# A two-hop graph product with layer norm: the products of steps 1 to 5 are issued one step earlier in TensorE's order

## The reference, cut to what matters

```python
adj = adjacent_mat((A + A.T) * 0.5)      # add the identity, scale rows and columns by deg ** -0.5
y = Coefficient2 @ adj                   # Coefficient2 is A, that is the raw input adj
y = y @ x
out = layernorm(x + y)
```

## Time and profile before

| | |
|---|---|
| median of three runs | 429.55 us |
| the profiled execution's own time | 428.08 us |
| its span | 426.3 us |
| PE busy | 393.6 us (92%) |
| DVE busy | 241.3 us (57%) |
| ACT busy | 111.6 us (26%) |
| POOL busy | 74.0 us (17%) |
| mean granted clock of PE | 0.974 of full speed |

### The profile page before, as it was taken

The page is one execution under the profiler, slowest core; times in us unless marked ns, Lnnn a source line. Parts: engine busy times, 40 slices in busy tenths (PEclk is TensorE's granted clock), DMA queues, the critical chain, the costliest instruction groups (busy, mean ns, idle before and its releaser), DMA issues.

```text
span 426.3 us, 5406 instructions
## 1 busy us (share of the span) xinstructions
PE 393.6 (92%) x1822; PEld 325.6 (76%) x1822; DVE 241.3 (57%) x463; ACT 111.6 (26%) x195; POOL 74.0 (17%) x109
## 2 busy tenths in 40 slices
PE   3479999997799699999999999999999999999994
PEld 3467788885588488888888888888888888888883
DVE  0656777773704402222266227777777777777752
ACT  1124444432603402222222222222222222222210
POOL 3466878752000000000000000000000000000000
PEclk9659999999999999999999999999999999999999
DMA  8999855430004736226232256565555555655500
GB/s 241 303 315 288 243 165 185 136 100 2 0 2 98 174 74 148 49 51 147 50 100 50 49 127 152 137 151 138 146 137 149 139 146 137 150 138 151 122 25 25
DMA packets 73969, 54.76 MB, mean 128 GB/s; under 512 B 3552, under 2 KB 62048, under 8 KB 73952
## 3 DMA queue, kind: packets, MB, share of 16 engines
q1 hardware_dynamic: 73952, 54.54, 49.8%
HBM read 41.94 MB, written 4.19 MB: 108 GB/s over the span
## 4 chain that ended last, share of the span: by engine, by line
issue 73%; PE 14%; DVE 7%; DMA 2%; SPq 2%; POOL 1%; ACT 0%; POOLq 0%; DVEq 0%
PE ps L412 3%; PE ps L391 3%; PE ps L393 3%; PE ps L392 3%; DVE lots_r L674 2%; DMA lots_s<-adj 2%; PE ps L420 1%; DVE u_lo L686 1%; POOL rstd L382 1%; DVE lots_s L633 1%; DVE store L633 1%; DVE deg L648 0%; SPq L284 0%; PE ps L435 0%; SPq L274 0%
## 5 line engine op out<-in xcount | busy, mean ns | idle before, releaser
L393 PE MATMUL ps<-z,w_lo 128*128 128x512 f32 x256 | 99.7, 389 | 0.0
L391 PE MATMUL ps<-z,w_hi 128*128 128x512 f32 x256 | 99.7, 389 | 0.0
L392 PE MATMUL ps<-z,w_hi 128*128 128x512 f32 x256 | 99.7, 389 | 0.0
L391 PE MATMUL ps<-u_hi,w_hi 128*128 128x512 f32 x176 | 69.4, 394 | 4.1 <-DVE z_raw L700 4.1
L616 ACT ACTIVATE w_hi<-turned 128x512 fp32r<-128x512 f32 x64 | 39.8, 632 | 122.9 <-DVE turned L741 122.9
L393 PE MATMUL ps<-u_hi,store_lo 128*128 128x512 f32 x176 | 69.3, 394 | 0.0
L392 PE MATMUL ps<-u_lo,w_hi 128*128 128x512 f32 x176 | 69.1, 392 | 0.0
L741 DVE STREAM_TRANSPOSE turned<-strips 128x512 f32<-128x512 f32 x64 | 65.5, 1069 | 0.0
L382 POOL TENSOR_TENSOR rstd<-var_eps,mhalf 128x1 f32<-128x1 f32 x16 | 8.8, 548 | 303.6 <-DVE var_eps L791 303.6
L700 DVE SCALAR_TENSOR_TENSOR z_raw<-ps,dinv_half,z_raw 128x512 fp32r<-128x512 f32 x16 | 11.9, 750 | 86.4 <-ACT z_raw L572 86.4
L391 PEld LDWEIGHTS ps<-z,w_hi 128*128 128x128 f32 x256 | 48.1, 188 | 10.0
(11 more groups left out here) (78 smaller groups left out, 432.7 us busy)
## 6 DMA issues: line engine op xcount, KB each, us to landing
strips<-adj SPq DMA_DIRECT2D x64, 256.0 KB, 4.5
z<-z_raw SPq DMA_DIRECT2D x64, 128.0 KB, 2.4
u_x<-x SPq DMA_DIRECT2D x16, 256.0 KB, 4.7
x_res<-x SPq DMA_DIRECT2D x16, 256.0 KB, 2.6
out<-y_out SPq DMA_DIRECT2D x16, 256.0 KB, 2.1
lots_s<-adj SPq DMA_DIRECT2D x13, 256.0 KB, 4.6
store<-adj SPq DMA_DIRECT2D x2, 512.0 KB, 5.7
col_slot<-adj SPq DMA_DIRECT2D x1, 896.0 KB, 9.8
```

What stands on the lines that cost most here:

```text
L391: nc.tensor.matmul(out_, hi, mov_hi, start=first, stop=False)
L392: nc.tensor.matmul(out_, hi, mov_lo, start=False, stop=False)
L393: return nc.tensor.matmul(out_, lo, mov_hi, start=False, stop=last)
```

## The change

A table `DONE_BY` says how many units PE has issued by the end of each step. Before, it was none by the end of step 1, then 5, 10, 15 and 20 by the ends of steps 2 to 5. Now it is 5, 10, 13, 17 and 21, and 25 by the end of step 6, as before; from there on the orders are alike. In step k the units of blocks up to k-2 still go between the chunks (`units_left`); those of block k-1 go behind the last chunk and mirror of the step (`late`). That makes 5 late units in step 1, 5 in step 2, 3 in step 3, 2 in step 4 and 1 in step 5.

On DVE, `lot_low` and `u_low` of block 0 (and the first `first_low`) stand behind the second add of step 1 and no longer behind its degrees; in steps 2 to 5 `lot_low` and `u_low` of block k-1 stand ahead of the degrees. The columns of step 1 take turns in both transposing banks, so that a chunk waits for the add of the chunk before the last.

```diff
@@ -250,6 +250,15 @@
         def main_parts(k):
             return sum(main_part(j) is not None for j in range(k))
 
+
+        DONE_BY = {1: 5, 2: 10, 3: 13, 4: 17, 5: 21}
+
+        def done_by(k):
+            return DONE_BY.get(k, max(0, (G + 1) * (k - 1)))
+
+        def bank_of(k, i):
+            return i % 2 if k < 2 else 0
+
         def hi_of(n):
             return w_next if n == 1 else w_hi[:, (n + 1) % 2 if n == 0 else n % 2]
 
@@ -406,10 +415,10 @@
                     last.then_inc(s_tc, 1)
 
             def transpose_cols(k, i, b0, b1):
-                pe.wait_ge(s_add, chunk_at(k) + i)
+                pe.wait_ge(s_add, chunk_at(k) + i - (k == 1 and i > 0))
                 for b in range(b0, b1):
                     src = row(k, b, b + 1) if b == k else col(k, b, b + 1)
-                    last = nc.tensor.transpose(tp[0][:, b - b0], src[:, 0], ident[:])
+                    last = nc.tensor.transpose(tp[bank_of(k, i)][:, b - b0], src[:, 0], ident[:])
                 last.then_inc(s_tc, 1)
 
             def mirror(k, n, i, b0, b1):
@@ -463,10 +472,14 @@
 
             pe.wait_ge(s_ident, 2)
             first_step()
+            units = [(j, m) for j in range(NB) for m in range(G + 1)]
             for k in range(1, NB):
                 cols_left = list(enumerate(chunks_of(k)))
                 mirrors_left = [(mirror_at(k - 1) + n, m) for n, m in enumerate(mirrors_of(k - 1))] if 2 <= k <= NR else []
-                units_left = list(range(G + 1)) if k >= 2 else []
+                quota = DONE_BY.get(k, (G + 1) * (k - 1)) - done_by(k - 1)
+                ripe = max(0, (G + 1) * (k - 1) - done_by(k - 1))
+                units_left, late = units[:min(quota, ripe)], units[min(quota, ripe):quota]
+                del units[:quota]
                 pe.wait_ge(s_in[k], 16 * ((k < NR) + (k < NB - 1) + 1))
                 summed = False
                 while cols_left or mirrors_left or units_left:
@@ -477,10 +490,12 @@
                         n, (i, b0, b1) = mirrors_left.pop(0)
                         mirror(k - 1, n, i, b0, b1)
                     if units_left:
-                        multiply_unit(k - 2, units_left.pop(0))
+                        multiply_unit(*units_left.pop(0))
                     if not summed:
                         col_sums(k)
                         summed = True
+                for unit in late:
+                    multiply_unit(*unit)
                 if k > NR:
                     mirror_corner(k - 1)
             for m in range(G + 1):
@@ -629,7 +644,7 @@
             def add_chunk(k, i, b0, b1):
                 dve.wait_ge(s_tc, chunk_at(k) + i + 1)
                 w = row(k, b0, b1)
-                bank = tp[i % 2 if k == 0 else 0]
+                bank = tp[bank_of(k, i)]
                 nc.vector.scalar_tensor_tensor(w, bank[:, 0:b1 - b0], 1.0, w, ALU.mult, ALU.add,
                                                accum_out=part_sum[:, k, i:i + 1]).then_inc(s_add, 1)
 
@@ -704,6 +719,13 @@
             for k in range(NB):
                 for i, (b0, b1) in enumerate(chunks_of(k)):
                     add_chunk(k, i, b0, b1)
+                    if k == 1 and i == 1:
+                        lot_low(0)
+                        u_low(0)
+                        first_low(0)
+                if 2 <= k < 6:
+                    lot_low(k - 1)
+                    u_low(k - 1)
                 degrees(k)
                 if k == 0:
                     nc.vector.tensor_tensor(c0[:, 0], c0[:, 0], ident2[:], ALU.add).then_inc(s_d0, 1)
@@ -714,11 +736,11 @@
                     nc.vector.tensor_tensor(diag, diag, ident2[:], ALU.add).then_inc(s_diagl, 1)
                 if k > NR:
                     corner_low(k - 1)
-                if k >= 1:
+                if k >= 6:
                     lot_low(k - 1)
                     u_low(k - 1)
-                    if k - 1 < len(FIRST):
-                        first_low(k - 1)
+                if 2 <= k <= len(FIRST):
+                    first_low(k - 1)
                 if k == NB - 2:
                     rest_low(0, range(2))
             lot_low(NB - 1)
```

## The result

The changed kernel takes 441.40 us (median of four runs, 440.46 to 442.43), the kernel before 430.19 (four runs, 429.06 to 432.80): a ratio of 1.0275, 95% interval 1.0235 to 1.0314. The forecast of 435.5 had the direction and half the size; the time lies at the upper edge of the range and is that of the clock rival.

What follows compares the result with a forecast made beforehand. PE, busy 92% of the span, was taken as slack early and nearly full later. Profiled 428.08 + 4.4 (later products) + 1.5 (clock) = 434.0, and 1.47 to the runs' median gives 435.5 us; range 428.5 to 441.5.

Steps and rivals of the forecast that it cites:

- the clock rival: The clock goes down in several steps, costing about half of 13.7 us: 441 us, chance 0.20.
- The direction and its mechanism: Steps 2 to 5: late units wait behind DVE's low lot and u_lo instead of running beside next step's columns; slower, 0.77.
- Step 1: First product at 21.2 us and not 26.72; step 2 begins at about 27.0, the clock rising 5.1 us after the product.
- the clock term: Steps 2 to 5: idle stretches may lower the clock; taken as 1.5 us, between 0 and 13.7.
- upper end of 13.7: All four steps 2 to 5 at 0.50 clock: 14 chunks by 0.51 and 33 products by 0.20, 13.7 us.
- 1.99 us from low lot to product: Steps 2 to 6: from the start of the lot's low part to the first product, 1.99 us each step.
- 68.9 - 27.0: First product of block 5 at 68.9 us, less step 2's start at about 27.0.
- 4.4 as forecast: First product of block 5 at 68.9 us instead of 64.47, moving the rest of the span by 4.4 us.
- The faster rival: PE is the bound; its 3.66 us of idle time in steps 1 and 2 go: 425.9 us, chance 0.13.
- No change: The lead of 1.1 us at step 3 is lost over steps 3 to 6: 429 us, chance 0.10.

Runs made afterwards that it cites:

- e1: The changed kernel with 33 matmuls that nothing reads filling PE's waits for u_lo in steps 2 to 5: 436.14 us, kernel before 429.84.
- e4: The changed kernel up to the end of step 2, no units in step 3, then the orders of the kernel before: 431.50 us, kernel before 429.84.
- e2: The changed kernel's step 1 alone; from step 2 on no late units and DVE's old order: 428.90 us, kernel before 429.84.
- e3: The kernel before with only DVE's order changed, low lot and u_lo ahead of the degrees in steps 2 to 5: 432.28 us, ratio 1.0063.
- g2: e2 with matmuls that nothing reads in four later waits of PE: 424.77 us, kernel before 430.00.
- g4: g2 with 28 transposes of the identity ahead of step 1: 424.22 us, kernel before 430.00.
- g3: The kernel before with matmuls that nothing reads in the same four later waits as g2: 426.70 us, kernel before 430.00.
- h1: g4 with the waits for u_lo of blocks 1 and 2 also filled by matmuls: 422.64 us, kernel before 430.08.

## Why the prediction had the direction and missed the size

- **The direction and its mechanism held.** The units of steps 2 to 5 stand behind DVE; the waits were foreseen as about 2.3 us twice and 1 to 2 us twice, and are 2.56, 2.56, 2.15 and 1.94. e1 and e4 show their cost without the clock's.
- **Step 1 held.** First product 21.16 (21.2); step 2 at 25.76 (27.0), as the clock rose 2 us behind the first product and not 5.1. It is earlier by 1.2, and that is luck of this execution: with the same step 1, step 2 began at 27.13 in e1 and at 27.22 in e4.
- **The step that failed is the clock term, "I take 1.5 us, half of one block of 15 products at half clock".** It measured 6.3 us by the marks of e1 and an estimated 6.7 by the stretches, about half of the upper end of 13.7, as the rival had it: the clock fell behind all four waits and not at half of one block. The reason given was a row in which PE waited 2.21 us at 1.00. e2 has the same wait in the same place, and the clock fell behind it. One such row of one execution shows that the clock can stay up, not that it does. The rule of the Trainium skill that the prediction weighed against this row ("TensorE: Matmul & The Clock Gate", "A second HAM failure mode: psum-queue depth-cycling") describes what the trace then showed: bursts with idle stretches between, and a clock that goes back and forth. That PSUM banks are the reason is not shown here: the four waits are for `u_lo`.
- **A second term was too small: 1.99 us from low lot to product.** It is 2.43, 2.42 and 2.42 in steps 2, 3 and 5. The 1.99 was read where the degrees gave ACT and POOL time to get ahead; the change takes that cover away. In step 4 it is 2.01, but there the low lot itself starts 0.59 us late, behind a mirror on PE that waits for ACT's copy (0.46 in e1's step 4). So steps 2 to 6 take 44.0 us at full clock, from step 2 to the first product of block 5, and not 68.9 - 27.0 = 41.9.
- **The sum, mended.** 4.4 as forecast + 2.1 for the longer line + 6.3 for the clock - 1.2 for the earlier step 2 = 11.6, the shift of the first product of block 5 in the profiled executions. From there on the two traces differ by 0.8 us.
- **The faster rival** named the real gain, but only of step 1: 3.0 us by step 10 in e2. **No change** fell with the waits: 9.21 us of them.

Open: why a wait of 2.56 us lets the clock fall in the changed kernel and not in e4, and how e3's 2.4 us split.

## What to carry to other kernels

Before moving a product up to where its operand is just made, count the whole chain behind that operand on the other engines, with the collisions that the old order happened to hide. Where PE will work in bursts with waits of one to three microseconds between them, price a stretch at half clock behind each wait as a case that may well come: here it came behind all four waits in the changed kernel's trace, and behind neither of the two rows of e4's. Then try matmuls into a free bank in those waits: on the kernel before this was worth 3.3 us, the early start at a held clock 1.9.

## What the runs showed of the chip

The granted clock fell behind waits of 1.4 to 2.6 us (1.43 in g2, 1.44 in g4, 2.22 in e2, 2.56 in the changed kernel) and then stayed at 1.2 GHz for 3.05 to 3.50 us in the stretches shown of the changed kernel and g4, with PE busy all the time. Waits as long left it at 2.4 GHz elsewhere: 1.41 and 2.56 in e4, 2.21 in the kernel before. So such a wait's price is its length, or its length and an estimated 1.5 to 1.8 us more (half of such a stretch), and which of the two isn't told by the wait alone. With matmuls without a use in the long waits the clock was at 1.00 over each stretch that had them (26.5 to 71.15 in e1, 98 to 160 in g2 and g3, 13 to 160 in h1), in one profiled execution each; what was left of the waits was up to 1.49 us (h1, for `z_raw`). All six executions of h1 have a mean granted clock of 0.996 or more.

A two-input DVE instruction of 128x512 and POOL's add beside it: the one that began later was the longer, `u_lo` 1.23 us for 0.74 alone, the low lot 1.27 for 0.69, POOL's add 1.75 for 1.30.
